# Deformable-convolution kernel: the 27 offset and mask columns by 96-column products, carried to their partitions through memory; two sets of statistics moved from VectorE to ScalarE

## What is computed

```
xdw   = depthwise3x3(x) + dw_b
om    = (xdw @ om_w + om_b).reshape(n, h, w, 32, 27)   # 9 taps x (dx, dy), then 9 masks
value = (x @ vp_w + vp_b).reshape(n, h, w, 32, 8)
sampled = bilinear(value, base + tap + offset)          # zero outside the image
out   = einsum('nhwgkc,nhwgk->nhwgc', sampled, mask) @ op_w
```

## Time and profile before

| what | value |
|---|---|
| median of 3 runs | 3862.06 us |
| profiled execution | 3859.76 us, span 3858.0 us |
| TensorE busy over the span | 3628.5 us (94%) |
| VectorE busy | 3510.0 us (91%) |
| ScalarE busy | 2286.0 us (59%) |
| moved by DMA | 470.35 MB, mean 122 GB/s |
| first layer ends, second begins | about 3400 us |

### The profile page before, as it was taken

The page is one execution under the profiler, slowest core; times in us unless marked ns, Lnnn a source line. Parts: engine busy times, 40 slices in busy tenths (PEclk is TensorE's granted clock), DMA queues, the critical chain, the costliest instruction groups (busy, mean ns, idle before and its releaser), DMA issues. The chain is left out here.

```text
span 3858.0 us, 90635 instructions
## 1 busy us (share of the span) xinstructions
PE 3628.5 (94%) x37696; PEld 2369.5 (61%) x37696; DVE 3510.0 (91%) x2757; ACT 2286.0 (59%) x4547; POOL 565.0 (15%) x412
## 2 busy tenths in 40 slices
PE   4899999999999999999999999999999999858998
PEld 2566666666666666666666666666666666623333
DVE  4899999999999999999999999989999999948776
ACT  5556665666666665666556666665566666235554
POOL 0011111101111111111111001111111111104444
PEclk9999999999999999999999999999999999979999
DMA  6454565445555555455545555555544554345563
GB/s 177 100 111 102 110 125 132 101 111 116 124 120 109 114 123 115 94 108 127 131 99 119 112 121 114 107 122 131 118 100 97 106 107 94 52 158 199 209 215 147
DMA packets 319939, 470.35 MB, mean 122 GB/s; under 512 B 37244, under 2 KB 242684, under 8 KB 313736
## 3 DMA queue, kind: packets, MB, share of 16 engines
q0 software_dynamic: 94080, 196.11, 28.4%
q1 hardware_dynamic: 224584, 266.07, 23.2%
q10 hardware_dynamic: 832, 2.10, 0.1%
HBM read 262.53 MB, written 67.41 MB: 86 GB/s over the span
## 5 line engine op out<-in xcount | busy, mean ns | idle before, releaser
L1026 DVE TENSOR_TENSOR pv<-val,wsum 128x2048 f32<-128x2048 f32 x800 | 1811.2, 2286 | 21.4 <-ACT xdw L557 14.6
L796 PEld LDWEIGHTS ps_add<-ident,pv 128*128 128x128 f32 x12800 | 1401.2, 142 | 356.0 <-issue 223.7
L796 PE MATMUL ps_add<-ident,pv 128*128 128x128 f32 x12800 | 1527.2, 275 | 70.9 <-DVE pv L1026 62.7
L751 PE MATMUL ps_om<-xdw,omw 128*32 128x256 f32 x13824 | 868.4, 384 | 30.4 <-ACT hat L587 29.4
L585 ACT ACTIVATE hat<-ps_om,omb 128x256 f32<-128x256 f32 x576 | 276.0, 479 | 551.2 <-PE ps_om L751 501.9
L979 DVE TENSOR_TENSOR prod<-hat,mwy 128x1536 f32<-128x1536 f32 (+1 forms) x384 | 526.0, 1397 | 82.9 <-DMA wsum<-prod 61.8
L472 POOL DMA_DIRECT2D wsum<-prod x192 | 226.0, 1254 | 2556.8 <-DVE wsum L979 2556.8
L751 PEld LDWEIGHTS ps_om<-xdw,omw 128*32 128x32 f32 x13824 | 391.2, 109 | 330.2 <-issue 95.5
L589 ACT ACTIVATE msk<-ps_om,omb 128x256 f32<-128x256 f32 x288 | 137.0, 476 | 401.4 <-PE ps_om L751 399.3
L965 DVE TENSOR_TENSOR mwy<-hat,msk 128x768 f32<-128x768 f32 x288 | 274.4, 953 | 94.3 <-ACT hat L599 94.3
L722 PE MATMUL ps_bg<-tri,diag 128*32 128x512 f32 x3024 | 346.5, 592 | 11.9 <-ACT tri L551 11.9
(11 more groups left out here) (134 smaller groups left out, 2622.7 us busy)
## 6 DMA issues: line engine op xcount, KB each, us to landing
wsum<-prod POOLq DMA_DIRECT2D x160, 768.0 KB, 7.1
tri<-in_x_dram SPq DMA_DIRECT2D x725, 128.0 KB, 2.9
win<-in_x_dram SPq DMA_DIRECT2D x144, 256.0 KB, 3.6
x<-xres SPq DMA_DIRECT2D x128, 256.0 KB, 5.1
xres<-in_x_dram POOLq DMA_DIRECT2D x124, 256.0 KB, 8.4
out_dram<-c_x SPq DMA_DIRECT2D x31, 1024.0 KB, 4.5
c_x<-x SPq DMA_DIRECT2D x30, 1024.0 KB, 5.3
c_box<-box_d SPq DMA_DIRECT2D x16, 1024.0 KB, 7.4
```

Of the source, the lines that this page charges most:

```text
L751: mm = nc.tensor.matmul(ps_om[G * q:G * q + G, (par + i) % 2, 0:TOK], omw[:, h, comp, :], xdw[:, j % 2, h, q, :], start=h == 0, stop=h == ...
L796: mm = nc.tensor.matmul(ps_add[:, tb, c, :], pv[:, (j + uv) % PBUF, c, P * tb:P * tb + P], consts["ident"][:, :], start=uv == 0 and c % 4 ...
L1026: nc.vector.tensor_tensor(pv[:, (j + uv) % PBUF, :, :].rearrange("p c (r w) -> p c r w", w=W), val[:, :, SR * j + u:SR * j + u + SR, v:v + ...
```

## The change

Three parts.

1. **Offsets.** The weights are laid out by tap (`omw_taps`), so that one product has 96 columns: 3 components x 32 groups. A tap is now 4 products of 512 positions (2 pairs of bands x 2 halves of the channels) into both banks of `ps_om`, issued four taps ahead instead of two. Their result has partition = component x group and is brought to partition = band x group through memory: ScalarE copies it with its bias to `om_cols` (`keep_offsets`, 96 x 1024, one buffer), SP stores it to `om_rows` in three DMAs (`store_offsets`, 4 slots), and one tap later loads it back as `om` (`load_offsets`, 128 x 768, two buffers). `hats` then reads `om` and works 512 wide.
2. **Statistics by ScalarE.** The bn_stats are gone from VectorE. ScalarE sums x minus a pivot and its square, by `accum_out`: four 1024-wide instructions a step for x2 (tap 1), and two 2048-wide ones for each half of a channel half of the next image (28 halves in all; taps 7 and 0).
3. **What follows from the buffers.** `acc` now lies in `xres`, only `acc_t` is left as a landing buffer for x ahead, `over` lies in `spare`. In tap 4 `summed` now comes after `hats` and `keep_offsets`. SP's loop over images is written out.

```
@@ sync @@
+                def store_offsets(n, j, k):
+                    t = (STEPS * n + j) * TAPS + k
+                    sp.wait_ge(om_kept, t + 1)
+                    for a in range(COMPS):
+                        sp.dma_start(om_rows[(TAPS * j + k) % KEPT_SLOTS, :, :, a, :].rearrange("q g t -> g q t"),
+                                     om_cols[G * a:G * a + G, :].rearrange("g (q t) -> g q t", q=Q)).then_inc(om_stored, 16)
+                def load_offsets(n, j, k):
+                    t, par = (STEPS * n + j) * TAPS + k, (j + k) % 2
+                    sp.wait_ge(om_stored, 16 * COMPS * (t + 1))
+                    at_least(sp, mwy_done, t - 1)
+                    sp.dma_start(om[:, par, :, :], om_rows[(TAPS * j + k) % KEPT_SLOTS].rearrange("q g a t -> (q g) a t"))\
+                        .then_inc(om_loaded[par], 16)
...
+                    for k in range(TAPS):
...
+                        if k + OFFSETS_AHEAD < TAPS or not last:
+                            store_offsets(*tap_ahead(n, j, k, OFFSETS_AHEAD))
+                        if k < 2 and not last:
+                            sp.wait_ge(bg_full, unit(n, j, f"dw{k}", NI) + 1)
+                            load_tri(n1, j1, 1, k)
...
+                        if k in (2, 3) and more:
+                            sp.wait_ge(bg_full, unit(n, j, f"dw{k}", NI) + 1)
+                            load_tri(n2, j2, 0, k - 2)
...
+                        if k + LOADS_AHEAD < TAPS or not last:
+                            load_offsets(*tap_ahead(n, j, k, LOADS_AHEAD))
@@ scalar @@
+                def keep_offsets(n, j, k):
+                    t = (STEPS * n + j) * TAPS + k
+                    act.wait_ge(om_full, t + 1)
+                    at_least(act, om_stored, 16 * COMPS * t)
+                    nc.scalar.activation(om_cols[0:OROWS, :], ps_om[0:OROWS, :, :].rearrange("p b t -> p (b t)"), ACT.Identity,
+                                         bias=omb[0:OROWS, k:k + 1]).then_inc(om_kept, 1)
...
+                    act.wait_ge(om_loaded[par], 16 * (TAPS * STEPS // 2 * n + (TAPS * j + k) // 2 + 1))
+                    d = om[:, par, 0:2, :]
+                    nc.scalar.activation(hat[:, par, :, 1, :], d, ACT.Abs).then_inc(abs_done, 1)
+                    nc.scalar.activation(hat[:, par, :, 0, :], d, ACT.Relu, scale=-1.0)
+                    nc.scalar.activation(hat[:, par, :, 2, :], d, ACT.Relu)
...
+                        if k + 2 < TAPS or not last:
+                            hats(*tap_ahead(n, j, k, 2))
+                        if k + OFFSETS_AHEAD < TAPS or not last:
+                            keep_offsets(*tap_ahead(n, j, k, OFFSETS_AHEAD))
                         if k == BACK_AT and not first:
-                            if j in (1, 2) and has_next(n):
-                                act.wait_ge(sums_made, CH * CH * n + CH * j)
                             summed(s - 1)
...
+                        if k == AHEAD_AT and j < CH and has_next(n):
+                            sums_ahead(n, j, 0)
+                        if k == 0 and j in (1, 2) and has_next(n):
+                            sums_ahead(n, j - 1, 1)
+                        if k == 1 and not is_step(n, j, 0, 0) and not is_step(n, j, 0, 1):
+                            statistics(*previous(*previous(n, j)))
@@ tensor @@
-                    at_least(pe, om_free, 3 * t + i - 1)
-                    comp = (2 * k, 2 * k + 1, 18 + k)[i]
-                    for h in range(CH):
-                        for q in range(Q):
-                            mm = nc.tensor.matmul(ps_om[G * q:G * q + G, (par + i) % 2, 0:TOK], omw[:, h, comp, :],
-                                                  xdw[:, j % 2, h, q, :], start=h == 0, stop=h == CH - 1)
+                    at_least(pe, om_kept, t)
+                    for tb in range(2):
+                        for h in range(CH):
+                            mm = nc.tensor.matmul(ps_om[0:OROWS, tb, :], omw[:, h, k, :],
+                                                  xdw[:, j % 2, h, 2 * tb:2 * tb + 2, :].rearrange("p q t -> p (q t)"),
+                                                  start=h == 0, stop=h == CH - 1)
```

More of the change, by code:

```diff
@@ L419, in step @@
                     more = not (isinstance(n, int) and n == NI - 1 and j >= STEPS - 2)
-                    if not first:
-                        sp.wait_ge(bg_full, step_unit(n, j, NI))
-                        load_window(n1, row_groups(j1)[0])
-                    for qp in range(2):
-                        sp.wait_ge(bg_full, unit(n, j, f"dw{qp}", NI) + 1)
-                        load_tri(n1, j1, 1, qp)
-                    if first:
-                        sp.wait_ge(bg_full, unit(n, j, f"first{V_UNITS - 1}", NI) + 1)
-                        load_window(n1, row_groups(j1)[0])
@@ L429, in step @@
-                    if not is_step(n, j, 0, 0) and not is_step(n, j, 0, 1):
-                        store_x2(*previous(*previous(n, j)))
-                    if more:
-                        for qp in range(2):
-                            sp.wait_ge(bg_full, unit(n, j, f"dw{2 + qp}", NI) + 1)
-                            load_tri(n2, j2, 0, qp)
-                    if j1 == 0:
-                        sp.wait_ge(bg_full, unit(n, j, f"value{V_UNITS - 1}", NI) + 1)
-                        load_window(n1, 1)
@@ L442, in _ @@
+                for n in range(NI):
+                    for j in range(STEPS):
+                        step(n, j, (n, j) == (0, 0), (n, j) == (NI - 1, STEPS - 1))
                 store_x2(NI - 1, STEPS - 2)
@@ L809, in _ @@
                 pe.wait_ge(weights_loaded, WL)
-                for k in range(2):
-                    for i in range(3):
-                        offsets(0, 0, k, i)
+                for k in range(OFFSETS_AHEAD):
+                    offsets(0, 0, k)
                 def step(n, j, first, last):
@@ L919, in _ @@
                 dve.wait_ge(diag_made, CH * CB * 3 + 1)
-                def sums_ahead(n, j, half):
-                    dve.wait_ge(x_ahead[half], 16 * (CH * n + j + 1))
-                    for i in range(HW // 1024):
-                        last = nc.vector.bn_stats(bs1[:, j, HW // 1024 * half + i, :], ahead[half][:, 512 * i:512 * i + 512])
-                    last.then_inc(sums_made, 1)
                 def scales_ahead(n, j, part):
@@ L1844, in layout @@
     per_block = lambda a: np.ascontiguousarray(np.tile(a, (Q, 1)))
+    by_tap = [c for k in range(TAPS) for c in (2 * k, 2 * k + 1, 2 * TAPS + k)]
     mean8 = np.kron(np.eye(P // GC), np.full((GC, GC), 1.0 / GC)).astype(np.float32)
```

220 lines of the change are left out of this document (125 added, 95 removed).

## The result

The changed kernel takes 4547.66 us (median of 4 runs, 4541.32 to 4554.85), the kernel before on the same chip 3860.76: a ratio of 1.178, 95% interval 1.176 to 1.180. That is 687 us slower where 574 had been forecast; the time lies in the given range, and 18 us beyond the 4350 to 4530 of the likeliest case.

A forecast was written before the change was run, and what follows sets the result against it. TensorE was taken to set the pace, VectorE some 4 us a step behind. Products 222, stall 295, clock 62, small ones -15 and start 10 gave +574 us on 3859.8, rounded to 4435 us, range 4200 to 4560.

The forecast's parts named there:

- Term 1: TensorE's offset products: a 96-column block takes 3.53 us instead of 2.76, over 288 taps +222 us.
- Term 2: TensorE's first add in tap 4 stands 9.8 us a step for ScalarE's late copy emptying ps_add: +295 us.
- The ring: Stores, six tri issues, load, hats and keep_offsets: a round of 12.2 us in taps 2 and 3, against 11.7 a tap.
- E3 = S3 + 10.7: ScalarE's keep_offsets in tap 3 ends 10.7 us after TensorE starts that tap.
- sign of error: Long waits elsewhere: on om_kept at a tap's head, or VectorE waiting for the accumulating DMA with TensorE idle.
- Term 3: TensorE's granted clock falls after each long stall, costing 2.0 us a step: +62 us, bounds 0 and 3.2 a step.
- Term 4: Small ones: VectorE's bn_stats relief -15 us, later start +10; ScalarE's sums over x and DMA cost nothing.
- the cover gone: If TensorE were no longer later than VectorE, the relief of 4.9 us a step would be worth 157 us.
- Short stall: Rival: only the unavoidable 3.1 us stall in tap 4 is left, clock untouched, +307, 4167 us; chance 0.22.
- products alone: Rival: the tap 4 stall hides altogether and only the offset products cost, +217, 4077 us; chance 0.05.
- DMA crowded: Rival: the load lands in 5 us or more among stores, tri loads and accumulations, 4500 to 4650 us; chance 0.10.
- VectorE the bound: Rival: TensorE only waits for pv, so VectorE's 4.9 us a step come home, about -160, 3700 us; chance 0.03.

The follow-up runs named there:

- e3: Changed kernel with the two ps_add copies first in ScalarE's tap 4 and load_offsets right behind store_offsets on SyncE: 4032.26 us, ratio 1.046.
- e1: Changed kernel with the two copies of summed moved ahead of hats and keep_offsets in ScalarE's tap 4: 4333.06 us, ratio 1.124.
- e2: Changed kernel with SyncE's load_offsets directly behind store_offsets, ahead of the six tri issues, window load and x2 store: 4231.70 us, ratio 1.098.
- e4: Changed kernel with both statistics back on VectorE, so the offsets part alone: 4582.71 us, ratio 1.187.
- e6: Offsets part alone (statistics on VectorE) with copies first in ScalarE's tap 4 and load_offsets right behind store_offsets: 4033.47 us, ratio 1.046.
- e7: Kernel before with statistics on ScalarE, the four x2 passes spread over two taps and VectorE's aggregate one tap later: 3857.80 us, ratio 1.000.
- two half-product kernels: e3 and e6, each with only 128 of 256 channels summed into the offsets: 3939.34 us from e3, 3901.68 us from e6.
- e8: Kernel before with only the sums over the next image's x on ScalarE, x2 statistics staying on VectorE: 3870.06 us, ratio 1.004.
- e5: Kernel before with the statistics part alone on ScalarE, the four x2 passes in one piece in tap 1: 3951.24 us, ratio 1.024.
- e3_half: e3 with half of the offset products, only 128 of 256 channels summed into the offsets: 3939.34 us, ratio 1.022.

## Why the prediction was right, and where it was off

**What bounds.** Right: TensorE set the pace, and both large costs came as work and standing of TensorE.

**Term 1, offset products**, mis-sized: +222 forecast, 174 measured by e3 against before (4032.26 less 3857.74). The block takes 3.43 us from start to start, not 3.53, which is 193 us for 288 taps. The rest came back in the `add` groups, whose busy time in e3 is 19 us less than before (1508.5 against 1527.2), perhaps because they are split by one offset group a tap instead of two; a depthwise tap went from 10.95 us (1640.74 to 1651.69 in the kernel before) to 11.5. The mechanism, three quarters of the columns filled, is argued from shapes; that the products cost this much more is shown. From the about 60 cycles of overhead that the Trainium skill, TensorEngine Tiling (Array Packing), Instruction Overhead, gives each matmul, the prediction had estimated 1.0 us back a tap. The runs don't show it: with 40 fewer records a tap TensorE is busy longer.

**Term 2, the emptied `ps_add`**, right in mechanism and nearly in size: 9.8 us a step forecast, 10.4 in the middle stretch and 313.3 us in 31 waits measured, where I had 304. e1 and e2 show both of its causes, the order on ScalarE and the ring.

The ring itself was mis-sized, and **this is the step that failed**: the rounds of taps 2 and 3 at 12.2 us, with "E3 = S3 + 10.7", a keep that ends inside its tap, and so no wait at the head of tap 4. Measured in the mean of the 25 steps, these rounds, into the keeps of taps 3 and 4, took 14.7 and 12.6 us, and the keeps of taps 1, 2 and 3 ended 10.0, 12.9 and 14.3 us behind the start of their tap instead of 7.2, 10.2 and 10.7. Of the 14.7, 6.7 lie between a keep's start and the issue of the load, where the sum had 5.4, 5.1 between issue and hats instead of 3.8, and 2.9 in the hats, as forecast. In the step shown the round into tap 3 lasted 13.6 us (keeps at 1615.86 and 1629.44), its load took 5.1 us (1621.41 to 1626.50), and the keep came 1.8 us too late for TensorE. So TensorE stood at the heads of taps as well: 120.0 us for `om_kept`, where before had 29.4 for hats, some 91 us for which the sum had no term; the text named such waits only as a sign of error. The two waits for the ring are 14.2 us a step in the middle stretch (341.6 us in 24 steps) where 9.8 were forecast; that the one at the `add` came so close is partly luck, since the other had taken lateness away ahead of it.

Two more readings of that sum were off. It let the x2 statistics hold tap 1, but e4 shows the same rounds without them, and in 17 of the 25 steps the hats behind them still waited for the load. And a median isn't the landing where it counts: the 3.8 us that I took is near the 3.9 of all loads, but those of the rounds into the keeps of taps 1 to 3 took 4.7 to 5.2. The formula of the Trainium skill, DMA: Bandwidth & Descriptors, Anatomy of one DMA, is given there for transfers that GpSimd issues; for this load, which SyncE issues, its estimated 2.9 us was too short.

**Term 3, the clock**, mis-sized: +62 forecast, bounds 0 to 99, and 109 us measured as busy time beyond e3's. Not only the 16 adds behind the long stall ran slow (3.58 us instead of 1.84): so did some groups behind the waits at tap heads, for which the sum had no term either (offset blocks behind waits of 2.23 to 6.55 us lasted 5.0 to 6.7 us, where 3.60 is usual). The middle stretch shows 0.94, not 0.97.

**Term 4, small ones**: -15 for VectorE. Between e4 and the changed kernel the same move is worth 35 us, between e6 and e3 nothing. In e7 a step is 0.4 us shorter in the profile, close to the 0.5 that I took, and the time is unchanged. The aside that the relief "would be worth" 157 us with the cover gone did not come true in the two half-product kernels: there it cost 38, since the ring took VectorE's place. That the sums over x would delay hats with a quicker load is not borne out: e3 and e6 tie, and in e8 they cost 12 us elsewhere. What delays hats in e5, where no load is in the way, are the passes over x2. The start was low: the first copy of `ps_add` in the changed kernel comes at 266.33 against 214.24, 52 us later and not 10; in e3 it is 7 later (220.98), so this too is the ring and the order.

In the balance of the two profiles: 163 for the products, 109 for the clock, 306 more of waiting for the copy (313.3 less 7.6), 91 for `om_kept`, and 26 of small waits of either sign make 695. The products were priced 59 us too high (222 against 163), and that covered a third of the 180 us that were missing elsewhere; the nearness of the total is to that extent luck.

**The rivals.** Short stall and products alone are excluded by the 10.4 us. Products alone became true in e3, at 4032 where 4077 was given. DMA crowded is in part right: of the two rounds that it names, the load of the first landed in 5.1 us in the mean, which is its "5 us or more", that of the second in 4.0. The time, 4548, lies in its 4500 to 4650 as well. But it can't stand for the whole: in e2, with the same transfers, 316 us came off, most of it, by the rows of the round into tap 3, through the place of the load's issue in the queue. What makes these landings long was not tested. VectorE the bound: e5 to e7 leave nothing of it.

## What to carry to other kernels

When data leaves an engine through memory and comes back, write down the whole ring, each issue that stands between store and load on the queue included, and follow it round by round against the consumer's periods, with the landing times of just those rounds; here one reordered load issue was worth 316 us of 687. One long round does no harm if its neighbours are short: in e2 the keep of tap 2 still starts 14.5 us behind the one before, but those of taps 1 and 3 only 11.5 and 9.9, and TensorE waits 8.5 us of the whole run at tap heads. A moved pass over data is priced by the lead that the neighbouring engine has at that place (buffers, banks), not by the busy share of the engine that takes it: the same four passes cost 94 us in one piece and nothing in two. And relief of an engine that is not the pace was worth little here, though it was 91% busy: nothing in e3 and e7, 35 us in the changed kernel.

## What the runs showed of the hardware

- The load of 384 KB landed in 3.9 us (median of 288, 2.9 to 9.3), but where it followed three stores and six `tri` loads in the queue, into the keeps of taps 1 to 3, in 4.7 to 5.2 us in the mean of 25 steps; ahead of the `tri` loads, in e2, in 4.2 to 4.7.
- The issue of three stores takes SyncE 1.27 us as a rule, but in the changed kernel 4.21 us at 1684.40, while GpSimd's accumulating transfers into `xres` were just issued (1678.41 to 1684.29); six `tri` issues took 2.84 us in the median of the changed kernel and up to 6.42, and 6.71 at 1677.96 of e3_half. A queue's issue time is not constant; the cause was not tested.

```profile
1684.40 4.21 SPq L408 DMA_DIRECT2D om_rows<-om_cols  x3
1688.71 1.70 SPq L416 DMA_DIRECT2D om<-om_rows  x1
```

- With a stall of 10 us in each step of 126 the granted clock of the middle stretch was 0.94, with 5.5 us 0.97, with none 0.99: what standing costs on top of itself was about a quarter here (109 us for 417 us of added idle).
